# Gated cross-attention and expert layer: search tables kept apart, first group reordered, 16-bit bounds

## What is computed

```python
x = x + tanh(g_xattn) * xattn(layernorm(x), ctx)     # 32 batches of 112 tokens, 256 wide, 16 heads
x = x + tanh(g_ffn) * ffn(layernorm(x))
# xattn: q,k,v projections with bias, RoPE on q and k, causal softmax, output projection
# ffn: statistics of x -> router hidden layer (gelu) -> 32 logits -> softmax, top 2 of 32 experts
#   every expert takes at most cap = int(1.25 * 3584 / 32) = 140 of its routed tokens, by probability
#   (ties by token number); xe = xf[idx]; hidden = silu(gate) * up; out += w * (hidden @ down)
#   16 adapters (one for two experts) get the same tokens, scaled by 0.05
```

## Time and profile before

| what | value |
|---|---|
| median of three timed runs | 783.05 us |
| the profiled execution | 782.0 us |
| its span | 780.2 us |
| PE busy | 678.5 us (87%) |
| DVE busy | 526.3 us (67%) |
| ACT busy | 405.6 us (52%) |
| POOL busy | 323.0 us (41%) |
| issue of the table's first transfer (L1193) | 2.23 us |
| first scores of group 0 | 28.91 us |
| first marks of list 0 | 486.98 us |
| first products of expert 0 | 507.12 us |

### The profile page before, as it was taken

One profiled execution on the slowest core, in us unless ns is written; L12 is line 12 of the kernel. 1 busy time (PEld: TensorE's weight loads), 2 busy tenths in 40 slices (PEclk: granted clock), 3 DMA queues, 4 the chain that ended last, 5 costly groups with the idle time before them and its releaser, 6 DMA issues.

```text
span 780.2 us, 17506 instructions
## 1 busy us (share of the span) xinstructions
PE 678.5 (87%) x5251; PEld 535.2 (69%) x5251; DVE 526.3 (67%) x1537; ACT 405.6 (52%) x1569; POOL 323.0 (41%) x339
## 2 busy tenths in 40 slices
PE   6899999999999999999897113499999999999993
PEld 3466666666666666666664102299999999999992
DVE  5654776777867678675898798767666566544441
ACT  1357788787788877787784465022222222222220
POOL 3243353443624446253112000335656656565642
PEclk9979999999999999999999555699999999999997
DMA  5600020110102002010101601149898898888921
GB/s 164 245 2 25 2 72 25 53 46 13 58 24 71 26 24 70 1 48 1 34 16 49 230 1 22 27 112 275 244 260 265 233 274 261 263 262 247 275 47 15
DMA packets 57723, 85.47 MB, mean 110 GB/s; under 512 B 11314, under 2 KB 28336, under 8 KB 57648
## 3 DMA queue, kind: packets, MB, share of 16 engines
q1 hardware_dynamic: 47456, 73.96, 28.7%
q0 software_dynamic: 9216, 9.76, 7.9%
q10 hardware_dynamic: 976, 0.89, 0.4%
HBM read 71.89 MB, written 12.69 MB: 108 GB/s over the span
## 4 chain that ended last, share of the span: by engine, by line
PE 54%; ACT 18%; DVE 17%; issue 6%; DMA 1%; POOL 1%; DVEq 1%; ACTq 1%; POOLq 0%
PE pair L965 20%; PE bank L975 10%; ACT arena L1270 8%; DVE arena L1438 5%; PE pair L1577 5%; PE bank L1542 3%; PE bank L1605 2%; PE pair L1586 2%; ACT arena L546 2%; PE pair L1572 2%; ACT arena L1218 2%; PE bank L987 2%; PE bank L1521 1%; ACT arena L1258 1%; PE bank L1535 1%
## 5 line engine op out<-in xcount | busy, mean ns | idle before, releaser
L1270 ACT ACTIVATE arena<-pair,arena 112x112 f32<-112x112 f32 x512 | 175.5, 365 | 61.5 <-DVE arena L1438 56.7
L965 PE MATMUL pair<-arena,we 128*128 128x140 f32 x1024 | 139.9, 286 | 0.6 <-ACT arena L875 0.6
L855 POOL DMA_INDIRECT rows_out<-arena,slot_row x64 | 94.4, 1475 | 97.3 <-DVE arena L906 79.3
L965 PEld LDWEIGHTS pair<-arena,we 128*128 128x128 f32 x1024 | 130.2, 192 | 0.9 <-issue 0.9
L883 ACT ACTIVATE arena<-pair 128x140 f32<-128x140 f32 x160 | 45.9, 287 | 152.3 <-PE pair L965 152.3
L918 DVE SCALAR_TENSOR_TENSOR arena<-arena,pair 128x140 f32<-128x140 f32 x160 | 47.6, 298 | 98.4 <-ACT arena L883 98.1
L1270 ACT ACTIVATION_READ_ACCUMULATOR arena<-pair,arena 112x1 f32 x512 | 109.9, 215 | 0.0
L844 POOL DMA_INDIRECT arena<-rows,slot_row x64 | 62.8, 981 | 93.6 <-issue 93.6
L975 PE MATMUL bank<-arena,we 128*128 128x140 f32 x512 | 83.4, 286 | 0.0
L1438 DVE TENSOR_REDUCE arena<-pair 112x8 f32<-112x896 f32 x64 | 68.9, 1077 | 18.0 <-PE pair L1577 17.1
L1586 PEld LDWEIGHTS pair<-tab,arena 112*112 112x112 f32 x512 | 52.2, 134 | 31.0 <-issue 29.2
(11 more groups left out here) (204 smaller groups left out, 1196.7 us busy)
## 6 DMA issues: line engine op xcount, KB each, us to landing
we<-w_experts_in SPq DMA_DIRECT2D x192, 256.0 KB, 4.2
wa<-w_adapters_in SPq DMA_DIRECT2D x16, 384.0 KB, 5.3
arena<-ctx_in SPq DMA_DIRECT2D x8, 448.0 KB, 4.4
arena<-x_in SPq DMA_DIRECT2D x8, 448.0 KB, 3.8
rows_out<-arena SPq DMA_DIRECT2D x8, 448.0 KB, 3.3
rows<-arena SPq DMA_DIRECT2D x8, 448.0 KB, 3.4
arena<-rows,slot_row POOLq DMA_INDIRECT x64, 4.0
rows_out<-arena,slot_row POOLq DMA_INDIRECT x64
```

Of the source, the lines that this page charges most:

```text
L855: nc.gpsimd.indirect_dma_start(d["out"], bass.IndirectOffsetOnAxis(ap=slot_row[:, h, e:e + 1], axis=0), yr[e % 2][:, h, :], None, compute_ ...
L965: last = nc.tensor.matmul(banks[m % 4][:, part * CAP:(part + 1) * CAP], w[:, col0:col0 + 128], xet[j % 2][:, c, :], start=(c == 0), stop=( ...
L1270: last = nc.scalar.activation(pr[s % 2][:, j, :], banks[BS[s % 4]][0:T, j * T:(j + 1) * T], ACT.Exp, bias=nmx[s // 2 % 2][:, s % 2, j:j + ...
```

## The change

1. The search's table (`srt`), `needed`, `same`, `half`, `shift`, `place` and `counts` get memory of their own outside the arena; `place` becomes one tile, `counts` and `bound` 16-bit. DVE makes the constants at step 2 of the last group (`search_setup`, `SETUP`). The search table is loaded in group 0, after the weights of experts 0 and 1.
2. ACT, PE and DVE no longer call `attention_done`; ACT and DVE wait on two semaphores instead (`rows_stored`), after the last logits' work.
3. `live[k]` is made by two tensor-scalar operations and one sum: clip(live - bound, -1, 1) * 2048 + digit.
4. The two bounds are made by three DVE instructions; the sum of the first two digits and its comparison move to `beside(10)`, in the first round of the third digit.
5. The tables for regrouping, spreading and summing are one 16-bit table `ways`; the matmuls at L596, L617 and L618 become 16-bit. List 0's bounds are spread first, into a bank of their own, and DVE starts list 0 on them; the other lists' bounds are copied behind list 0's counting.
6. The first group goes K0, K1, V0, X0, X1, Q0, Q1, V1, with fixed banks (`BANKS_FIRST`), `keep_warm` 3 after X1 and 14 after V1. The layer norm's statistics stand ahead of the waits for gates and biases on DVE, its application ahead of the first rotation. wv has a semaphore of its own. `gbo` (the gated output bias) is made after the rotations. Before `scores` DVE rotates Q for batch 0 alone (`rotate_first`); batches 1 to 3 are rotated in steps 0 and 1 of group 0, and `scores` waits for them at batch 1.
7. PE runs `keep_warm(2)` between the bases of list 1 and the first rows of the experts.

The diff's core:

```diff
@@ -66,7 +66,7 @@
...
 IDLE = {7: 24, 12: 7, 14: 2}
-ABOVE = float(2 << DBITS)
+ABOVE, NOWHERE = float(2 << DBITS), float(3 << DBITS - 1)
@@ -199,9 +202,10 @@
...
-FRONT_FIRST = [(0, "K", 0), (2, "K", 1), (4, "X", 0), (5, "X", 1), (6, "Q", 0), (7, "Q", 1), (9, "V", 0), (10, "V", 1)]
-ROTATE_FIRST = (1, 4, 7, 8)
-WARM_FIRST = {("K", 1): 12, ("X", 1): 1}
+FRONT_FIRST = [(0, "K", 0), (1, "K", 1), (2, "V", 0), (4, "X", 0), (5, "X", 1), (6, "Q", 0), (7, "Q", 1), (9, "V", 1)]
+ROTATE_FIRST = (0, 1, 6, 7)
+WARM_FIRST = {("X", 1): 3, ("V", 1): 14}
+LN1_FIRST, BIAS_FIRST = 0, 8
@@ -233,6 +237,8 @@
...
+SETUP = 2
@@ -260,6 +266,8 @@
 BS, BO, BM = (0, 1, 2, 3), 4, (5, 6, 7)
+BANKS_FIRST = {("K", 0): BM[0], ("K", 1): BM[1], ("V", 0): BM[2], ("X", 0): BS[2], ("X", 1): BS[3],
+               ("Q", 0): BM[0], ("Q", 1): BM[1], ("V", 1): BO}
@@ -457,6 +467,11 @@
...
+    def rows_stored(eng):
+        for s in (s_xout, s_xfc):
+            eng.wait_ge(s, GV[s])
@@ -531,8 +546,8 @@
...
-        attention_done(act)
         shifted_exp(LATE, len(EARLY_ROWS) + 1)
+        rows_stored(act)
@@ -560,7 +575,6 @@
...
     def routing_tensor(pe):
-        attention_done(pe)
@@ -593,10 +607,11 @@
...
         for g in range(LISTS):
-            last = nc.tensor.matmul(banks[5][:, 2 * g:2 * g + 2], lay[:, LAY["spread"]][:, g * 128:(g + 1) * 128], bound,
-                                    start=True, stop=True)
-        last.then_inc(s_spread, 1)
-        list_bases(pe, 0, banks[5][:, 16:18])
+            out = banks[4][:, 8:10] if g == 0 else banks[5][:, 2 * g - 2:2 * g]
+            last = nc.tensor.matmul(out, ways[:, WAY["spread"] + g, :], bound, start=True, stop=True)
+            if g in (0, LISTS - 1):
+                last.then_inc(s_spread, 1)
+        list_bases(pe, 0, banks[4][:, 16:18])
@@ -614,8 +629,8 @@
         pe.wait_ge(s_counted, g + 1)
-        nc.tensor.matmul(out, lay[:, LAY["before"]], counts[:, g, 1:3], start=True, stop=False)
-        nc.tensor.matmul(out, lay[:, LAY["chunk"]], counts[:, g, 0:2], start=False, stop=True).then_inc(s_base, 1)
+        nc.tensor.matmul(out, ways[:, WAY["before"], :], counts[:, g, 1:3], start=True, stop=False)
+        nc.tensor.matmul(out, ways[:, WAY["chunk"], :], counts[:, g, 0:2], start=False, stop=True).then_inc(s_base, 1)
@@ -677,20 +692,22 @@
...
-    def routing_vector(dve, link):
-        attention_done(dve)
+    def search_setup(link):
...
         for g in range(LISTS):
-            nc.vector.tensor_copy(place[g][:, LT:], tab[:, TAB["seek"]])
+            nc.vector.tensor_copy(place[:, g, LT:], tab[:, TAB["seek"]])
...
+    def routing_vector(dve, link):
...
         dve.sem_inc(s_scr, 1)
+        rows_stored(dve)
@@ -704,6 +721,10 @@
...
+            if n == 2 * ROUNDS:
+                link(nc.vector.tensor_tensor(low[1], found[:, 0:1], found[:, 1:2], ALU.add))
+                link(nc.vector.tensor_scalar(low[0], low[1], 2.5, NOWHERE, ALU.is_lt, ALU.mult))
@@ -722,9 +743,10 @@
...
                 top = found[:, k - 1:k]
-                nc.vector.tensor_scalar(over, live[k - 1], top, ABOVE, ALU.is_gt, ALU.mult)
-                link(nc.vector.scalar_tensor_tensor(live[k], live[k - 1], top, digit[k], ALU.is_equal, ALU.mult))
-                link(nc.vector.tensor_tensor(live[k], live[k], over, ALU.add))
+                link(nc.vector.tensor_scalar(over, live[k - 1], top, 1.0, ALU.subtract, ALU.min))
+                link(nc.vector.tensor_scalar(over, over, -1.0, ABOVE, ALU.max, ALU.mult))
+                link(nc.vector.tensor_tensor(live[k], over, digit[k], ALU.add))
@@ -744,20 +766,23 @@
...
                        s_cand, (ROUNDS + 1) * k + r + 2)
-            link(nc.vector.tensor_scalar(found[:, k:k + 1], bound_at(ROUNDS), -1.0, None, ALU.mult))
-        link(nc.vector.tensor_reduce(low, found, X, ALU.add))
-        link(nc.vector.tensor_scalar(low, low, DIGITS + 0.5, 2 * ABOVE, ALU.is_lt, ALU.mult))
-        nc.vector.tensor_copy(bound[:, 0:1], found[:, DIGITS - 1:DIGITS])
-        link(nc.vector.tensor_tensor(bound[:, 1:2], found[:, DIGITS - 1:DIGITS], low, ALU.add))
+            if k < DIGITS - 1:
+                link(nc.vector.tensor_scalar(found[:, k:k + 1], bound_at(ROUNDS), -1.0, None, ALU.mult))
+        nc.vector.tensor_scalar(bound[:, 0:1], bound_at(ROUNDS), -1.0, None, ALU.mult)
+        link(nc.vector.scalar_tensor_tensor(low[1], bound_at(ROUNDS), -1.5, low[0], ALU.is_gt, ALU.mult))
+        link(nc.vector.tensor_tensor(bound[:, 1:2], bound[:, 0:1], low[1], ALU.add))
...
         dve.wait_ge(s_spread, 1)
-        link(nc.vector.tensor_copy(bound_of.rearrange("p g k -> p (g k)"), banks[5][:, 0:2 * LISTS]))
-        for part in range(RANKS):
-            list_part(dve, link, 0, part, list_bank(0), banks[5][:, 16:18])
+        link(nc.vector.tensor_copy(bound_of[:, 0, :], banks[4][:, 8:10]))
+        list_part(dve, link, 0, 0, list_bank(0))
+        dve.wait_ge(s_spread, 2)
+        link(nc.vector.tensor_copy(bound_of[:, 1:, :].rearrange("p g k -> p (g k)"), banks[5][:, 0:2 * (LISTS - 1)]))
+        for part in range(1, RANKS):
+            list_part(dve, link, 0, part, None, banks[4][:, 16:18])
@@ -1026,6 +1052,7 @@
...
         list_bases(pe, 1, banks[7][:, 0:2])
+        keep_warm(2, ident[0:T, 0:T], tab[0:T, 0:NT])
@@ -1069,6 +1097,7 @@
...
                     load_pair(0, 0)
+                    nc.sync.dma_start(srt, d["search"]).then_inc(s_dig, 16)
@@ -1082,9 +1111,8 @@
...
         attention_done(sp)
-        nc.sync.dma_start(srt, d["search"]).then_inc(s_dig, 16)
         nc.sync.dma_start(lay, d["lists"]).then_inc(s_lay, 16)
-        nc.sync.dma_start(regroup, d["regroup"]).then_inc(s_lay, 16)
+        nc.sync.dma_start(ways, d["ways"]).then_inc(s_lay, 16)
@@ -1339,18 +1367,22 @@
...
-        def rotate_all(z):
-            wait(dve, s_proj, z + 1)
-            dve.wait_ge(s_rope, 2)
-            nc.vector.stream_shuffle(prot[z % 2], proj[z % 2],
+        def rotate_first(z, some):
+            n = some.stop - some.start
+            cols = slice(some.start * T, some.stop * T)
+            dve.wait_ge(s_proj, z + 1)
+            dve.wait_ge(s_rope, z - 1)
+            nc.vector.stream_shuffle(prot[z % 2][:, cols], proj[z % 2][:, cols],
                                      mask=[i + DH // 2 if i % DH < DH // 2 else i - DH // 2 for i in range(32)])
-            by_batch = lambda a: a.rearrange("p (b t) -> p b t", b=GB)
-            each = lambda name: tab[:, TAB[name]].unsqueeze(1).to_broadcast([128, GB, T])
+            by_batch = lambda a: a[:, cols].rearrange("p (b t) -> p b t", b=n)
+            each = lambda name: tab[:, TAB[name]].unsqueeze(1).to_broadcast([128, n, T])
             link(nc.vector.tensor_tensor(by_batch(pcos[z % 2]), by_batch(proj[z % 2]), each("cos"), ALU.mult))
-            dve.sem_inc(s_rot, 1)
+            if some.stop == GB:
+                dve.sem_inc(s_rot, 1)
             link(nc.vector.tensor_tensor(by_batch(prot[z % 2]), by_batch(prot[z % 2]), each("sin"), ALU.mult))
-            nc.vector.tensor_tensor(qt[0][:, z - 2, :], pcos[z % 2], prot[z % 2], ALU.add).then_inc(s_rope, 1)
+            last = nc.vector.tensor_tensor(qt[0][:, z - 2, cols], pcos[z % 2][:, cols], prot[z % 2][:, cols], ALU.add)
+            last.then_inc(s_rope if some.stop == GB else s_q0, 1)
@@ -1458,7 +1492,9 @@
...
                     ln2_apply(g - 1, 1 - par)
-                if front and s == (LN1_APPLY if prev or not own else LN1_SECOND[1]):
+                if own and not front and s == SETUP:
+                    search_setup(link)
+                if front and s == (LN1_FIRST if not own else LN1_APPLY if prev else LN1_SECOND[1]):
@@ -1468,7 +1504,13 @@
...
                     else:
-                        rotate_all(z)
+                        rotate_first(z, slice(0, 1))
+                if front and not own and s == BIAS_FIRST:
+                    dve.wait_ge(s_bo, 16)
+                    nc.vector.tensor_scalar(gbo, gbo, gates[0:T, 0:1], None, ALU.mult).then_inc(s_gate, 1)
+                if own and not prev and s < 2:
+                    rotate_first(2 + s, slice(1, GB))
@@ -1486,16 +1528,14 @@
...
+        ln1_stats(0)
...
         nc.vector.tensor_scalar(bqk[:, 2:4], bqk[:, 2:4], DH ** -0.5, None, ALU.mult).then_inc(s_gate, 1)
-        ln1_stats(0)
...
         nc.vector.tensor_copy(causalb, tab[0:T, TAB["causal"]]).then_inc(s_setup, 1)
-        dve.wait_ge(s_bo, 16)
-        nc.vector.tensor_scalar(gbo, gbo, gates[0:T, 0:1], None, ALU.mult).then_inc(s_gate, 1)
@@ -1507,8 +1547,12 @@
...
         def item(q, par, loads, kind, what, j, n, first, tail, between):
-            out = banks[BM[n % 3 if first else kind]]
-            wait(pe, s_mf[kind], n - 2 if first else FIRST[kind] + len(KINDS[kind]) * q + n)
+            out = banks[BANKS_FIRST[what, j] if first else BM[kind]]
+            if not first:
+                wait(pe, s_mf[kind], FIRST[kind] + len(KINDS[kind]) * q + n)
+            elif what == "Q":
```

(13 more changed lines are left out.)

85 lines of the change are left out of this document (46 added, 39 removed).

## The result

The changed kernel takes **770.01 us** (median of 4 runs, 769.12 to 772.08), the kernel before 782.16 us in the 4 runs taken with it (780.02 to 783.71): ratio 0.985, 95% interval 0.982 to 0.988. Forecast were 771.4 us and faster. The profiled execution took 769.41 us with a span of 767.6, 12.6 us less than before.

| step | forecast, us | measured, us |
|---|---|---|
| E: start to the last hidden row | -2.5 | -3.11 |
| A: last hidden row to the first search step | -3.4 | -3.87 |
| B: digits; `beside(10)` | -1.2; +0.1 | -1.28; +0.13 |
| C: last bound to the bases of list 0 | -2.6 | -2.78 |
| D: end of the lists to the end of expert 0's 24 products | -1.5 | -1.57 |

What follows compares the result with a forecast made beforehand. PE bounds the experts from 520 us on; ahead of them one chain of waits runs through one engine at a time. The terms -3.4 -1.2 +0.1 -2.6 -0.5 -1.5 -2.5 sum to -11.6 us: 783.05 becomes 771.4 us, range 767 to 777.

Steps and rivals of the forecast that it cites:

- E: First group: first scores at 23.2 us, -5.7, partly given back in group 0; net -2.5 us, bounds +1.2 and -6.
- A: Waits and constants ahead of the last logits: removing the list and moving the constants gives -3.4 us, bounds -3.0 and -3.7.
- B: Search digits: two 16-bit tensor-scalar operations and a sum, -0.58 us twice, -1.2 us; `beside(10)` costs +0.1 us.
- C: From bound to list 0: fewer small operations, 16-bit matmuls for spreading and bases; -2.6 us, bounds -2.2 and -2.9.
- D: Start of the experts: `keep_warm(2)` keeps PE's clock up for the first 24 products; -1.5 us, bounds -1.7 and +0.3.
- Rival 3: Waits taken out are replaced by others ending as late, and 16-bit matmuls cost as fp32; 776.0 us, chance 0.08.
- rival 2: Clock at the experts doesn't change the time: fall comes anyway or the median never had it; 772.9 us, chance 0.20.
- +1.2 for V0 at the lower level: Group 0: PE idles 4 us before V0 of group 1, which at the lower clock takes 3.6 us; +1.2 us.
- The rest of the experts: Bases of lists 2 and 3, among the PE-bound experts: four passes become two, -0.5 us for both, bounds 0 and -0.8.
- Rival 1: First group gives everything back: scores start earlier, but rotations and a low clock eat it; 773.9 us, chance 0.22.
- Rival 4: Slower: longer idle time before V0 in group 0 takes the clock down for most of the group; 786.5 us, chance 0.03.

Runs made afterwards that it cites:

- fp32 experiment: Changed kernel with spreading of the bounds and the bases of all four lists in fp32 again, new order kept; 774.11 us, ratio 0.990 to the kernel before.
- the rotation behind the maxima: Changed kernel with the other three batches of the second query row rotated in step 2 of group 0, behind the second maxima; 773.00 us, ratio 0.991.

## Why the prediction was right, point by point

**A** was forecast at -3.4 us and is -3.79 at the maxima. The logits did start 0.06 us behind the hidden row, and DVE followed them at once, but I had them take 1.16 us and DVE start another 0.15 later; they took 0.97, all at the upper clock, which before fell while they ran (at 428.6 us). That the constants had to be moved is the one point in which the case shows less than the step suggests: behind the removed waits DVE has 1.25 us to spare. They did fit at step 2 (DVE's idle time ahead of the earlier logits' maxima there is 0.17 us instead of 1.55), but not for nothing: with them there DVE idles 0.51 us ahead of L1438 of the last group, where it idled 0.15 before, and the 0.36 us are absent in both profiles with the constants back (and in the one with the old first group). That is as much as leaving them behind the attention costs (0.31). Taking the waits out was it. Rival 3 (other waits take their place) is out.

**B** was right in kind and size: 0.63 us per digit against the 0.58 forecast, since the second operation took 0.39 us instead of 0.45. Putting the old operations back costs 1.28 us, so nothing was hidden there. `beside(10)` costs 0.13 us.

**C**, forecast -2.6, is -2.78, and the fp32 experiment divides it as 1.2 for the data and 1.6 for the rest. I had counted most of the 1.65 us of the spreading as the 16-bit matmul's; with wide data in the new order DVE waits only 0.40 us longer, so the larger part belongs to the order.

**D** was right for the case that the profile shows: 1.67 us less in the 24 products, 0.1 lost ahead of them, and the fall returns to the hundredth when the warm matmuls go. I gave rival 2 (clock without effect) 0.20 because the moment of a change might vary between runs. It does, at places that I had not looked at. The Trainium skill, "TensorE: Matmul & The Clock Gate", Part 1, says that this moment differs between runs of the same kernel; the three profiles of the changed kernel agree, with the clock low for 3.4, 6.9 and 3.4 us in group 0. Between edits it differs in more places: Q takes 3.24 us, but 4.9 in two of them, and the second warm block 2.51 us, but 4.1 to 4.6 in five. In those five the experts start 1.2 to 1.8 us later and the warm matmuls stand in their way; whether the unedited kernel does this in some of its runs, none of its profiles shows. By my estimate every median here carries 1 to 3 us that no edit explains.

**E** is the term that was mis-sized, -2.5 against -3.11 at the last hidden row. That the two lie so close is partly luck: at the fourth maxima it was -5.58, and 2.5 us were lost behind them in places that I had not foreseen. The first scores were right (23.2 forecast, 22.6 measured, Q at the upper clock), and so was what comes back by the second maxima (2.0 forecast; the maxima lag 2.24 further behind the scores than before). The step that failed is "+1.2 for V0 at the lower level". V0 did run at the lower clock (3.12 us, forecast 3.6), but part of it had done so before (2.46), so the cost was 0.66; and DVE's application behind it lay beside less of POOL's work and took 2.00 us instead of 2.62, which gave 0.62 back. The third maxima kept the 4.0 us of the second. Then the clock, low for 10.3 us of group 0 before, was low for 3.4, and the gain grew to 5.58; I had put that only into the lower bound. It depends on the execution: in the second profile of the changed kernel the clock was low for 6.9 us, and 5.04 were left at the fourth maxima. The delay from DVE through ACT to V0, which I had drawn, is there; that the operation behind V0 stretches beside POOL I had left out.

Then 1.4 us of the gain went away in the loop of groups. In every second group DVE is idle 0.54 us ahead of L1451, the router's count of small values, where it was idle 0.17, the same instructions otherwise. From DVE's timelines, of the changed kernel and of the one with the old first group:

```profile
158.66 0.42 DVE L1451 TENSOR_SCALAR_CACHE_REDUCE we<-we 112x256 f32<-112x256 f32 x1 [0.54 <-DVE arena L1445]
```

```profile
162.67 0.42 DVE L1445 TENSOR_SCALAR_CACHE_REDUCE we<-we 112x256 f32<-112x256 f32 x1 [0.17 <-DVE arena L1439]
```

Three trips of the loop at 0.36 us each, and the 0.36 of the last group told under A, give the 1.4. The three come with the new first group: all twelve profiles that have it show 0.54 and 0.53 us there, and the one with the old first group 0.17, as before. They are a price of E that I did not count. Which of its edits brings them, and by what mechanism, no run tests. The fall of the clock at 417 us took the remaining 1.03: the profiles without the warm matmuls at the experts and with the rotation behind the maxima don't have this fall, and lose nothing there.

**The rest of the experts** gained 0.1 us and not 0.5. The fp32 experiment gives 0.34 for the bases, within the bounds, and the other profiles of changed kernels end 0.5 us sooner than the one of the result, a difference that arises behind the 150th microsecond of the experts and is none of the change's.

**The range** was 767 to 777, but the terms that I named for its ends give 768.0 (E at -6) and 777.7 (E at +1.2, D at 0, one microsecond more). The result lies within both.

**Rival 1** (the first group gives everything back): with the old first group the last hidden row is 2.6 to 3.2 us later and the median 775.2 us. Out. Against the kernel before, the old first group with the rest of the change gains 4.8 us in the median, the changed kernel 8.4 to 12.3; of that distance the marks of the one profile explain 2.6 to 3.2 and the 1.6 of the late rise. **Rival 4** (slower through the clock in group 0) did not happen in any profile of the changed kernel, but the warm matmuls in group 0 produced it on a small scale. My 0.03 for it rested on the argument that PE has no long pauses behind V0, and that holds only as long as V0 itself fills the pause before the application.

## What to carry to other kernels

Ask of every wait in a list whether it is still needed at that place; one list of waits taken off the path gave 3.1 us by itself, and with the list gone the work moved from behind it gave nothing more. Before you speed up one engine in a stretch where three take turns, follow what releases each operation, and look at what runs beside it: here POOL's chain ended last but one edit that started it 2.3 us earlier moved the maxima by 0.16, while DVE work that started earlier beside it ran slower. A pause of PE can cost its clock. Filling one removed the fall ahead of expert 0; filling another, in group 0, moved the fall to the next pause, in front of work bound by PE. Read edits of a microsecond at their marks in the profile, not in medians whose runs spread over three. And look once through the stretches that you did not touch: 1.4 us went away there.

## What the runs showed of the hardware

DVE's in-place fp32 tensor-scalar on 112x256 (four of them) took 1.38 us with POOL idle, and 1.65, 2.00, 2.88 and 3.87 us the more of it lay beside POOL's 128x448 products. A sum of two 128x336 fp32 tensors took 0.51 us with POOL idle and 1.32 beside such a product. A 16-bit tensor-scalar over 896 columns took 0.46 and 0.39 us where the scalar-tensor-tensor took 1.15. The granted clock fell behind pauses of PE of 1.60, 1.80 and 2.19 us in three profiles. In the stretch from 72 to 75 us it stood at 1.00 in the changed kernel's second profile and at 0.57 with the rotation behind the maxima, where it fell at 71.2 us, although PE was busy 2.45 and 2.40 us from 69 to 72: nearly the same work with and without a fall.
